# A transformer block on one core: weights and context laid out transposed by the host, first batch's work moved ahead of the rest of the setup

## What is computed

```python
x = x + attn(layernorm(x), ctx, ctx, tau, delta, Wq, bq, Wk, bk, Wv, bv, Wo, bo)   # 16 heads of 16
x = x + ffn(layernorm(x), w1, conv_w, conv_b, w2)      # ternary weights: round(w / mean|w|) in [-1, 1]
x = x + window_attn(ctx, layernorm(x), lens, p_t, W_a, W_c)      # gaussian window, tanh(cat @ W_c.T)
x = x + moe(layernorm(x), W1, b1, W2, b2, Wr, br)      # 8 experts, top 1, 256 -> 1024 -> 256
```

## Time and profile before

| | |
|---|---|
| median of 3 runs | 580.57 us (579.96 to 581.64) |
| span of the profiled execution | 575.1 us, 5.5 us less than the median |
| mean granted TensorE clock | 0.824 |
| PE busy | 407.0 us, 71% |
| DVE busy | 303.8 us, 53% |
| ACT busy | 176.3 us, 31% |
| POOL busy | 115.0 us, 20% |
| DMA | 64.42 MB, 112 GB/s over the span |

### The profile page before, as it was taken

How to read it: one execution, slowest core, us unless ns; L and a number is a source line. 1 busy time by engine, 2 the same in 40 slices (tenths; PEclk the granted TensorE clock), 3 DMA queues, 4 the chain that set the end, 5 groups by cost and what they waited for, 6 DMA issues and landing times. The chain is left out here.

```text
span 575.1 us, 7947 instructions
## 1 busy us (share of the span) xinstructions
PE 407.0 (71%) x2743; PEld 288.6 (50%) x2743; DVE 303.8 (53%) x820; ACT 176.3 (31%) x398; POOL 115.0 (20%) x130
## 2 busy tenths in 40 slices
PE   4525634948789789879778857816651299999995
PEld 3314424536566676666655736605431045656554
DVE  3783500775875966958958859537324011212121
ACT  2223122444453454453644613503011011111010
POOL 2966201300320221123013110100013201010101
PEclk9977857959969969799799896975565599999999
DMA  8454956554665472271551621198632401011100
GB/s 226 101 136 90 197 115 119 188 136 109 184 142 153 134 146 79 87 135 55 128 114 43 142 63 37 44 342 287 177 128 72 154 1 50 22 52 28 36 17 12
DMA packets 52953, 64.42 MB, mean 112 GB/s; under 512 B 12797, under 2 KB 45552, under 8 KB 52912
## 3 DMA queue, kind: packets, MB, share of 16 engines
q1 hardware_dynamic: 37916, 43.89, 31.9%
q10 hardware_dynamic: 13828, 17.23, 9.3%
q0 software_dynamic: 1168, 2.76, 1.5%
HBM read 49.40 MB, written 14.99 MB: 112 GB/s over the span
## 5 line engine op out<-in xcount | busy, mean ns | idle before, releaser
L569 PE MATMUL ps<-W 125*32 125x112 f32 (+2 forms) x1280 | 102.8, 290 | 33.0 <-DMA W<-d_nm 15.1
L569 PEld LDWEIGHTS ps<-W 125*32 125x32 f32 (+2 forms) x1280 | 71.5, 139 | 56.7 <-issue 17.0
L573 PE MATMUL ps<-idf,hold 128*128 128x128 f32 (+4 forms) x288 | 48.5, 296 | 60.2 <-DVE hold L1483 19.1
L569 PE MATMUL ps<-W,hold 128*128 x264 | 86.2, 470 | 4.4 <-DVE hold L1891 4.4
L1591 DVE TENSOR_REDUCE mx<-ps 112x1 f32<-112x375 f32 x128 | 61.5, 540 | 26.1 <-PE ps L569 25.8
L573 PEld LDWEIGHTS ps<-idf,hold 128*128 128x128 f32 (+4 forms) x288 | 36.6, 158 | 75.0 <-issue 27.9
L1012 ACT ACTIVATE hold<-ps 128x224 f32<-128x224 f32 (+4 forms) x80 | 33.1, 429 | 109.8 <-PE ps L573 76.8
L569 PEld LDWEIGHTS ps<-W,hold 128*128 128x128 f32 x264 | 47.9, 191 | 26.7 <-issue 22.7
L1161 ACT ACTIVATE W<-ps 125x448 f32<-125x448 f32 x96 | 44.9, 545 | 31.5 <-PE ps L569 31.5
L1374 POOL TENSOR_TENSOR rstd<-ve,expo 112x1 f32<-112x1 f32 x32 | 18.3, 573 | 136.2 <-DVE ve L1483 136.2
L1312 ACT ACTIVATE hold<-ps 128x512 f32<-128x512 f32 x22 | 13.1, 598 | 102.2 <-PE ps L569 102.2
(11 more groups left out here) (157 smaller groups left out, 596.9 us busy)
## 6 DMA issues: line engine op xcount, KB each, us to landing
W<-in_L_ffn_W ACTq DMA_DIRECT2D x16, 1024.0 KB, 9.7
hold<-in_ctx SPq DMA_DIRECT2D x16, 375.0 KB
d_k<-W SPq DMA_DIRECT2D x8, 562.5 KB, 4.4
W<-d_k SPq DMA_DIRECT2D x8, 562.5 KB
hold<-d_mask SPq DMA_DIRECT2D x8, 492.2 KB, 3.7
d_xs<-hold SPq DMA_DIRECT2D x1, 3598.0 KB, 21.6
hold<-d_xs SPq DMA_DIRECT2D x12, 257.0 KB, 2.7
W<-d_k SPq DMA_DIRECT2D x8, 375.0 KB
```

The costliest lines, as they stand in the source:

```text
L569: return pe.matmul(o, lhsT=l, rhs=r, start=start, stop=stop, skip_group_check=True)
L573: return pe.transpose(o, i, ident[0:n, 0:n])
```

## The change

The host now lays out `WqT`, `WkT`, `WvT`, `WoT`, `WcT`, `w1T`, `w2T` and `ctxT` transposed, and packs the identity matrix, all small biases, conv weights, `Wr` and tau in one array `consts` of 128 rows. All transposes of weights and context on PE and their copies on ACT go. `cxT` has four buffers and is filled by a DMA of SP (`p_ctx`). The rows of ones come from an array in DRAM by four small DMAs. The quantization works on the transposed weights: two passes on DVE for each, and a cast on ACT (`w_cast`) in place of the third pass, transposes and copies. `w_sum`, `w_mask`, `w_quant`, `w_bo`, `w_eb` and the writes of the mask stand later in the streams.

```diff
             for i in range(-1, B + 3):          # SP
-                w_eb(i)
+                if i < 2:
+                    p_ctx(i + 2)
+                if i >= 3:
+                    p_ctx(i + 1)
                 p_rows(i + 2)
                 u_mask(i - 1)
                 a_stack(i)
                 p_stackk(i + 1)
                 u_store(i - 2)
-                w_mask(i + 1)
                 p_stackq(i + 1)
+                w_mask(i)
                 u_cx(i - 1)
+                w_eb(i)
...
+            def p_ctx(b):
+                if b >= 4:
+                    sp.wait_ge(v_ps, b - 3)
+                    sp.wait_ge(sc_ps, b - 3)
+                sp.dma_start(cxT[b % 4][:, :, :], A["ctxT"][b]).then_inc(cxT_loaded[b % 4], 16)
...
+            rows(0)                             # SP, ahead of the loop
+            p_ctx(0)
+            sp.dma_start(WkT[:, :, :, :], A["WkT"]).then_inc(wk_loaded, 16)
             sp.dma_start(prep8[:, 0, :], A["fside_BxS2_0"]).then_inc(prep_loaded, 16)
...
+            for i in range(2):
+                sp.dma_start(kst32[i][KD:KX], A["ones"][:, 0:NH * L // 2]).then_inc(ones_loaded, 16)
+                sp.dma_start(qst32[i][KS:KD], A["ones"][:, 0:NH * T // 2]).then_inc(ones_loaded, 16)
+            for i, n in enumerate(("w1T", "w2T")):
+                sp.dma_start(nat_f[i], A[n]).then_inc(f_loaded, 16)
             sp.wait_ge(delta_made, 1)
             sp.dma_start(d_delta, prepb[:, :, :]).then_inc(delta_written, 16)
             sp.wait_ge(delta_written, 16)
-            sp.wait_ge(filled, 2)
...
                 pe.wait_ge(xn0T_sb, b + 1)      # PE, p_k
+                pe.wait_ge(cxT_loaded[b % 4], 16 * (b // 4 + 1))
...
             for i in range(-1, B + 3):          # ACT
-                w_gauss(i)
                 t_center(i - 2, 0)
...
                 p_qm(i)
+                w_gauss(i)
+                w_cast(i - 1, 0)
+                w_cast(i - 1, 1)
                 a_exp(i - 1, 2)
...
             for i in range(-1, B + 3):          # POOL
-                w_fill(i, 2)
-                w_fill(i, 3)
+                w_fill(i + 1, 2)
+                w_fill(i + 1, 3)
...
-                for n in range(0, 4):
-                    w_eb(i, n)
-                w_fill(i + 1, 1)
                 p_kr(i + 1)
                 p_kl(i + 1)
                 p_x0b(i)
+                for n in range(0, 4):
+                    w_eb(i, n)
...
             for i in range(-1, B + 3):          # DVE
                 for n in range(3, 6):
                     a_max(i - 1, n)
-                for n in range(0, 3):
-                    w_sum(i, n)
-                w_mask(i)
                 t_xq(i - 2)
-                w_bo(i - 1)
-                w_quant(i, 0, 0)
+                w_sum(i - 1, 2)
+                w_quant(i - 1, 0, 0)
+                w_quant(i - 1, 0, 1)
                 u_al(i - 3)
                 for n in range(6, 10):
                     a_max(i - 1, n)
-                w_quant(i, 0, 1)
-                w_quant(i, 0, 2)
+                w_bo(i - 1)
                 a_max(i - 1, 10)
                 t_h(i - 2, 0)
                 for n in range(11, 14):
                     a_max(i - 1, n)
-                w_quant(i, 1, 0)
+                w_quant(i - 1, 1, 0)
+                w_quant(i - 1, 1, 1)
                 a_max(i - 1, 14)
                 a_max(i - 1, 15)
...
                 p_ln(i + 1)
-                w_quant(i, 1, 1)
+                w_small(i + 1)
+                w_mask(i)
+                w_sum(i, 0)
+                w_sum(i, 1)
```

More of the change, by code:

```diff
@@ L23, in pixart_block @@
     NG = NH // HG
-    F0 = A["L0_ffn_w1"].shape[0]
+    F0 = A["w1T"].shape[1] // DC
     M0 = F0 // 128
@@ L166, in pixart_block @@
         amc = hb(128, T)
-        cxT = [None] * 3
-        for n in range(3):
-            cxT[(B + n) % 3] = hb(128, DC, L)
+        cxT = [None] * 4
+        for n in range(4):
+            cxT[(B + n) % 4] = hb(128, DC, L)
         FREE = used[0] - DC * L
@@ L277, in pixart_block @@
         const_loaded = sem("const_loaded")
-        cxT_ps = sem("cxT_ps")
-        cxT_sb = sem("cxT_sb")
-        cx_loaded = sem("cx_loaded")
+        cxT_loaded = [sem(f"cxT_loaded{i}") for i in range(4)]
+        wk_loaded = sem("wk_loaded")
+        wqv_loaded = sem("wqv_loaded")
+        wlate_loaded = sem("wlate_loaded")
         cxt_loaded = sem("cxt_loaded")
@@ L609, in w_tr @@
             @batch
[L610 to L644, removed]
             def p_cxT(b):
                 if b == 0:
-                    pe.wait_ge(qkvT_sb, 3)
-                    pe.wait_ge(bk4_made, 1)
-                pe.wait_ge(cx_loaded, 16 * (b + 1))
+                    pe.wait_ge(const_loaded, 16)
                 if b >= 1:
@@ L774, in t_h @@
             def t_h(b, half):
+                if b == 0 and half == 0:
+                    pe.wait_ge(quant, 2)
                 pe.wait_ge(xqT_sb, b + 1)
@@ L1024, in _ @@
-            for n, (w, dst) in enumerate(((1, WkT), (0, WqT))):
-                act.wait_ge(tr_qkv, n + 1)
-                for k in range(DC):
-                    last = copy(dst[:, k, :, :].rearrange("p m (d h) -> p m d h", h=HM),
-                                ps[:, w, k * D:k * D + D].rearrange("p (m h d) -> p m d h", m=DC, h=HM))
-                last.then_inc(qkvT_sb, 1)
-            act.wait_ge(tr_qkv, 3)
-            copy(WvT[:, :, :].rearrange("p k d -> p (k d)"), ps[:, 2, :]).then_inc(qkvT_sb, 1)
@@ L1191, in t_center @@
             def t_center(b, half):
-                if b == 0 and half == 0:
-                    act.wait_ge(const_loaded, 16 * 8)
                 act.wait_ge(h_evac, 2 * b + half + 1)
@@ L1327, in _ @@
             pool.wait_ge(ones_made, 1)
-            for m in (idf, idb):
-                last = pool.affine_select(out=m[:, :], in_=m[:, :], compare_op=ALU.not_equal, fill=1.0, base=0,
-                                          pattern=[[-1, 128]], channel_multiplier=1)
-            last.then_inc(idents, 1)
             pool.affine_select(out=tri, in_=tri, compare_op=ALU.is_gt, fill=0.0, base=0,
@@ L1338, in w_fill @@
                 if b == 0:
-                    pool.wait_ge(filled, n)
-                    if n == 1:
-                        pool.wait_ge(ln_rstd[0], 1)
-                        for i in range(2):
-                            pool.memset(kst[i][96:128, :, :], 1.0)
-                            last = pool.memset(qst[i][96:128, :, :], 1.0)
+                    pool.wait_ge(filled, n - 1)
                     if n == 2:
@@ L1933, with heads, chunks @@
         aps[name] = nc.dram_tensor(f"in_{name}", a.shape, _mybir.dt.from_np(a.dtype), kind="ExternalInput").ap()
+    f = {n: _np.asarray(a) for n, a in inputs.items()}
+    def heads(a):
+        return a.reshape(2, 8, 16, -1).transpose(0, 2, 1, 3).reshape(256, -1)
+    def chunks(a):
+        return a.reshape(-1, 128, a.shape[-1]).transpose(1, 0, 2)
+    cols = [_np.eye(128, dtype=_np.float32), chunks(heads(f["L0_xcond_bq"])), chunks(heads(f["L0_xcond_bk"])),
+            chunks(f["L0_xcond_bv"].reshape(-1, 1)), chunks(f["L0_ffn_conv_w"].reshape(1024, 3)),
+            chunks(f["L0_ffn_conv_b"].reshape(-1, 1)), chunks(f["L1_ffn_Wr"]), _np.tile(f["condB_tau"], (128, 1)),
+            _np.tile(f["L0_xcond_bo"], (128, 1)), _np.tile(f["L1_ffn_br"], (128, 1))]
+    laid = {"consts": _np.concatenate([c.reshape(128, -1) for c in cols], axis=1),
+            "WqT": chunks(heads(f["L0_xcond_Wq"]).T).reshape(128, 2, 2, 128),
+            "WkT": chunks(heads(f["L0_xcond_Wk"]).T).reshape(128, 2, 2, 128),
+            "WvT": chunks(f["L0_xcond_Wv"].T), "WoT": chunks(f["L0_xcond_Wo"].T), "WcT": chunks(f["L1_xcond_W_c"].T),
+            "w1T": chunks(f["L0_ffn_w1"].T).reshape(128, -1), "w2T": chunks(f["L0_ffn_w2"].T).reshape(128, -1),
+            "ctxT": f["ctx_1024"].transpose(0, 2, 1).reshape(8, 2, 128, 375).transpose(0, 2, 1, 3)}
+    laid["ones"] = _np.full((3, 3000), 0x3F803F80, _np.uint32).view(_np.float32)
+    for name, a in laid.items():
+        a = _np.ascontiguousarray(a)
+        arrays[f"in_{name}"] = a
+        aps[name] = nc.dram_tensor(f"in_{name}", a.shape, _mybir.dt.from_np(a.dtype), kind="ExternalInput").ap()
     out = nc.dram_tensor("out_x", inputs["x"].shape, _mybir.dt.float32, kind="ExternalOutput").ap()
```

213 lines of the change are left out of this document (67 added, 146 removed).

## The result

| | before | after |
|---|---|---|
| median, 4 runs each on one chip | 580.27 us (579.88 to 581.64) | 590.45 us (587.62 to 592.33) |
| ratio | 1 | 1.0178, 95% interval 1.0128 to 1.0228 |
| span of the profiled execution | 575.1 us | 585.9 us |
| mean granted TensorE clock | 0.824 | 0.795 |
| PE busy | 407.0 us | 400.4 us |

What follows compares the result with a forecast made beforehand. The loop was taken as bound by a chain of rounds through DRAM (K write and read-back, scores, maxima). Terms -14.3 + 12.9 + 4.2 = +2.8 gave a span of 577.9, plus 5.5 a time of 583.4 us; range 573 to 591.

Steps and rivals of the forecast that it cites:

- Setup, T0 at 40.0: Up to batch 0's first scores (T0): K write at 20.3 plus 19.7; 12.7 us gained, bounds 8 to 14.
- that slower rival: Setup: SP waits for `d_delta` until 25, so setup gives 8 in place of 12.7; 588 us, chance 0.14.
- T0 to the K write of batch 1, 25.9: From batch 0's first scores: 25.9 in place of 27.5, 1.6 us gained, bounds -0.4 to 4.8.
- passes and locks: Among batch 0's maxima: quantization passes and bias steps with DVE and POOL blocking each other, 7.0 us added, 7.9 at most.
- T1 to the K write of batch 2, 32.3: From batch 1's first scores (T1): fill, expert load and queue delay the maxima; 32.3 against 18.9, 12.9 us lost by T2.
- T2: Start of batch 2's first scores, 139.29 us before the change; T7 is the same mark for batch 7.
- The rival that the fill delays little: Batch 1's maxima: expert load does not lengthen the fill, write comes after 23, not 30.7; 575.7 us, chance 0.22.
- The other iterations, 4.2 lost: Rest of the loop: late `ctxT` in batches 4 to 7 costs 5.7, less 1.5; bounds 1.5 gained to 8 lost.
- The credit of 1.5: Other iterations: removed transposes counted as 0.8 us for all, the removed ACT copy as 0.7.
- These 5.5: Time around the span, 5.5 us, added to the predicted span of 577.9 to give 583.4.
- The rival that `ctxT` arrives in time: Batches 4 to 7: the K products do not wait, 5.7 us less; 577.7 us, chance 0.13.

Runs made afterwards that it cites:

- quant_late: Changed kernel with the four quantization passes moved behind the maxima and the two casts behind batch 0's last exponentials; ratio 1.0056 to the kernel before.
- bias_early: Changed kernel with POOL's four bias steps moved ahead of the K split of batch 1; ratio 1.0149 to the kernel before.
- fill_early: Changed kernel with the 3598 KB fill issued behind Q of batch 0, out of the bias step; ratio 1.0007 to the kernel before.
- ctx_early: Changed kernel with every context load issued a whole round ahead, nothing else; ratio 0.9934 to the kernel before.
- all_whole: Changed kernel with contexts a round ahead, bias steps early, quantization and casts late, whole fill behind batch 0's queries; ratio 0.968 to the kernel before.

## Why the prediction came out as it did

The sign and the place of the losses were right and 590.45 lies in the range, by 0.55 us at its upper end, but the kernel was slower by 10.2 us in place of 2.8. The size of the loop's term was wrong, as told below. By the steps of the prediction:

- **Setup, T0 at 40.0.** Measured 39.10. The K product started at 7.97 (8.8 predicted), the K write at 18.88 (20.3), and from there to T0 it took 20.2 (19.7). The wait for `d_delta` did not hold SP until 25, so that slower rival is out. It ended at 18.03, and POOL's last step of the K split at 18.67: two paths that the prediction had at 20.3 and 19.8 ended within 1 us of one another again. The 20.3 was a choice between 16 and 28, so that it came this close is partly luck.
- **T0 to the K write of batch 1, 25.9.** Measured 26.6. To the end of `nmT` it took 23.9, where 24.2 was predicted with 7.0 for passes and locks. quant_late takes 3.7 off the way to `nmT` and bias_early 3.3; with both moved, `nmT` is done 16.1 to 17.0 after T0, so passes and locks (the waits of DVE and POOL for one another) together cost 6.9 to 7.8. What the bounds had not named is that the locks also catch the tiny operations on the maxima (2.46 for a cast that takes 0.17 alone).
- **T1 to the K write of batch 2, 32.3.** Measured 31.9. fill_early shows that this is the fill: without it T1 to T2 is 9.5 shorter. The expert load lengthened the fill by 4.2 (27.3 against 23.1), where 5.5 was summed; what the context load, x and the mask add was not measured by itself. The rival that the fill delays little is out.
- **The other iterations, 4.2 lost.** This is the term that was mis-sized: 12.5 lost in the profiles of before and after; late contexts alone cost 13.0 in the mean of six against six. The mechanism was the one predicted, and the landing too: the K product followed L469's issue by 6.6 to 7.0 us in the four batches (6.3 predicted). The error of 8.3 has three parts. The direct waits were 8.0 in place of 5.7: batches 4 and 5, for which I guessed 1.6 together, waited 1.41 and 2.14. The credit of 1.5 for removed transposes and a copy shows nowhere: where the contexts are in time, T2 to T7 is 198.7 on average, no shorter than the 198.4 and 195.2 before (1.5 is less than what such marks move by, so this is no proof that it is nothing). And I priced a wait at its own length, without the time for which TensorE runs slower after it. The stretches of the changed kernel around the wait of 2.35:

```profile
262.00:266.00 4.00, 2.52 (x12) 1.32 (x10) 3.14 (x8) 1.31 (x4) 0.00 (x0) 1.00 0.57 172
266.00:270.00 4.00, 3.01 (x6) 1.78 (x7) 1.12 (x5) 0.00 (x0) 0.55 (x1) 0.70 0.03 12
```

and of ctx_early at the same place, where PE goes on without a gap:

```profile
252.00:256.00 4.00, 3.68 (x15) 2.07 (x13) 3.57 (x11) 1.69 (x4) 0.55 (x1) 1.00 0.38 128
```

PE had been at 2.4 GHz (1.00) until the wait; behind it the granted clock is 0.70, and the K product takes 4.48 us in place of 2.69: a wait of 2.35 cost 4.1. Batch 7 is alike: a wait of 2.06 and a product of 4.15. But the wait of 2.14 ahead of batch 5's product, at 224.50, left the clock where it was:

```profile
220.00:224.00 4.00, 2.23 (x11) 1.19 (x9) 3.42 (x8) 1.31 (x4) 0.00 (x0) 1.00 0.54 172
224.00:228.00 4.00, 3.28 (x11) 1.82 (x11) 1.34 (x6) 0.67 (x2) 0.55 (x1) 1.00 0.00 0
```

Its product took 2.79, and so did that of batch 4 behind a wait of 1.41. So a wait of about 2 us cost its own length in two batches and nearly twice that in the other two, and its length alone does not say which. The two long products are 3.1 us of the 4.5 that waits and credit leave open. In the mean of the runs 13.0 us were lost for 9.4 of waits, so some 3.6 came on top; PE's products took 4.5 us longer in the same runs. That all of it follows from the waits is not shown: all_whole ran at a clock of 0.83 from T2 to T7 with no such wait and took 203.0.

The sum with the measured sizes is -13.8 (T1) + 11.4 (T1 to T2) + 12.5 + 0.7 (tail) = +10.8 in the span, and 4.5 in place of 5.5 from the span to the median. These 5.5 were taken for what lies around the span, which they are not: each execution whose time and span are both on record has 1.7 to 1.9 around it. The rest is that the profiled execution was faster than the median one (587.62 against 590.45 for the changed kernel). The rival that `ctxT` arrives in time was wrong for this kernel but priced well: it gave 577.7, and ctx_early, which makes it true, gives 0.9934 x 580.57 = 576.7. In this rival the mis-sized term is absent, and the rest of the sum was right within the 2 us of that run's interval.

## What to carry to other kernels

A load that replaces on-chip work must be issued as early as the work it replaces had its input: here four loads behind the wrong neighbour in one queue turned a gain of 0.7% into a loss of 1.8%, and exchanging two neighbouring issues repaired it. Bulk traffic such as a fill belongs where the chain makes no round through DRAM for longer than it takes (24 us for a fill of 19.7 here), and whatever others wait for (a small write with two waiters) must not be queued behind it. Price a wait on the critical engine with and without a lower clock behind it: here four waits of 1.4 to 2.4 us cost their length twice and nearly double twice.

## What was not expected of the hardware

- A DMA's issue is not always short: 13.55 us for the `ctxT` load behind a fill of 3.6 MB with an expert load beside it, 8.47 behind the fill alone, 0.33 to 0.50 elsewhere. SP issues its next DMA only behind it. The kernel before has the same behind its fill, and the issue of x that follows took 5.34 there:

```profile
55.71 9.00 SPq L422 DMA_DIRECT2D hold<-in_ctx  x1
```

- Tiny operations are held as long as large ones. An operation of 112x16 on DVE took 2.46 and 1.84 us beside POOL's subtractions and 0.17 and 0.18 without them.
- Two context loads issued 0.4 us apart depend on their order: the one of 128 partitions landed after 3.3 us (median) in front of the one of 125 partitions and after 6.2 behind it.
